# Fp16 spreading of attention weights, and a first expert chunk that is weighted later, in a one-core attention and expert block on Trainium2

## The reference

```python
# neighbourhood attention, 16 heads of 8 channels, 13 neighbours (K)
qkv = (x @ qkv_w.T + qkv_b)...;  q, k, v = qkv[0] * SCALE, qkv[1], qkv[2]
attn = einsum('bhld,bhlkd->bhlk', q, k[:, :, nbr, :]) + rpb[:, bidx][None]
attn = softmax(attn, axis=-1)
out = einsum('bhlk,bhlkd->bhld', attn, v[:, :, nbr, :]) @ proj_w.T + proj_b
# experts: a GRU with 1024 states over the 512 steps gives the routing vectors
routing = l2norm(hs.reshape(B, S, E, D));  expr = (x @ expr_w.T).reshape(B, S, E, D)
gram = einsum('bsed,bsfd->bsef', routing, routing);  diff_n = l2norm(gram - eye(E))
penalty = mean(sum(diff_n ** 2))
cos_dist = 1 - sum(expr * routing) / (|expr| * |routing|)
scores = cos_dist * (1 + penalty)
top_v, top_i = top_k(scores, 2);  mult = softmax(top_v)
moe = sum over e of weight[e] * (silu(x @ gate_w[e].T) * (x @ up_w[e].T)) @ down_w[e].T
out = moe + the same form with the shared weights
```

## Time and profile before

| | us |
|---|---|
| median of 3 runs | 4211.66 |
| lowest, highest | 4198.45, 4226.81 |
| the profiled execution | 4216.87 |
| its span (first to last instruction) | 4215.0 |

### The profile page before, as it was taken

The page is one execution under the profiler, slowest core; times in us unless marked ns, Lnnn a source line. Parts: engine busy times, 40 slices in busy tenths (PEclk is TensorE's granted clock), DMA queues, the critical chain, the costliest instruction groups (busy, mean ns, idle before and its releaser), DMA issues. The chain is left out here.

```text
span 4215.0 us, 179359 instructions
## 1 busy us (share of the span) xinstructions
PE 3881.9 (92%) x76838; PEld 2507.1 (59%) x76838; DVE 3103.6 (74%) x14963; ACT 1509.4 (36%) x5111; POOL 161.7 (4%) x399
## 2 busy tenths in 40 slices
PE   3999589999999999999999999999999999987999
PEld 3777455656665666566665665656666656654665
DVE  2688677777777777777777777777777777776555
ACT  1112333333333444333333333333333334432222
POOL 1221000000000000000000000000000000000000
PEclk9899789999999999999999999999999999988999
DMA  2010400000000000000000000000000000010000
GB/s 67 18 37 35 155 3 3 3 3 3 3 3 3 3 3 3 3 3 3 3 3 3 3 3 3 3 3 3 3 3 3 3 3 3 3 36 8 10 10 12
DMA packets 46472, 51.44 MB, mean 12 GB/s; under 512 B 11668, under 2 KB 39572, under 8 KB 45716
## 3 DMA queue, kind: packets, MB, share of 16 engines
q1 hardware_dynamic: 45716, 40.48, 3.1%
HBM read 36.28 MB, written 4.19 MB: 10 GB/s over the span
## 5 line engine op out<-in xcount | busy, mean ns | idle before, releaser
L886 PE MATMUL psum<-room,h_parts 128*32 128x384 f16 x65536 | 2770.7, 327 | 137.5 <-DVE h_parts L1015 137.5
L886 PEld LDWEIGHTS psum<-room,h_parts 128*32 128x32 f16 x65536 | 1663.9, 97 | 1161.0 <-DVE h_parts L1015 359.9
L971 DVE STREAM_TRANSPOSE turned<-psum 128x128 f32<-128x128 f32 x1024 | 323.6, 316 | 524.2 <-PE psum L886 524.2
L1075 ACT ACTIVATE r_by<-gates 128x32 f32<-128x32 f32 x1024 | 253.2, 247 | 1154.3 <-DVE gates L950 1154.3
L747 DVE CUSTOM_DVE_ANT_0 products<-routes 128x128 f32<-128x128 f32 x1855 | 478.4, 270 | 5.0 <-ACT routes L740 3.0
L998 DVE TENSOR_TENSOR_SCAN state<-w_by,state 128x96 f32<-128x96 f32 x1024 | 366.4, 358 | 129.3 <-ACT state L1081 0.7
L1084 ACT ACTIVATE state<-state 128x32 f32<-128x32 f32 x1024 | 255.3, 249 | 434.7 <-DVE state L998 434.7
L989 DVE TENSOR_TENSOR_SCAN pre_n<-r_by,n_terms 128x96 f32<-128x96 f32 x1024 | 366.5, 358 | 22.9 <-ACT r_by L1075 2.3
L950 DVE TENSOR_TENSOR gates<-turned 128x32 f32<-128x32 f32 x2048 | 375.2, 183 | 0.0
L981 DVE STREAM_TRANSPOSE n_terms<-psum 128x128 f32<-128x128 f32 x1024 | 332.6, 325 | 0.0
L1081 ACT ACTIVATE state<-pre_n 128x32 f32<-128x32 f32 x1024 | 258.7, 253 | 136.6 <-DVE pre_n L989 3.4
(11 more groups left out here) (157 smaller groups left out, 2661.5 us busy)
## 6 DMA issues: line engine op xcount, KB each, us to landing
xs_room<-in_L_ffn_gru_w_hh_dram SPq DMA_DIRECT2D x16, 1536.0 KB, 7.1
room<-in_L_attn_x_dram SPq DMA_DIRECT2D x8, 256.0 KB, 5.4
x_scratch<-room SPq DMA_DIRECT2D x8, 256.0 KB, 2.3
room<-x_scratch SPq DMA_DIRECT2D x32, 64.0 KB, 2.2
out_dram<-room SPq DMA_DIRECT2D x32, 64.0 KB, 2.0
xs_room<-in_L_ffn_gru_w_ih_dram SPq DMA_DIRECT2D x3, 512.0 KB, 5.5
xs_room<-in_L_ffn_gate_w_dram SPq DMA_DIRECT2D x2, 512.0 KB, 6.1
xs_room<-in_L_ffn_up_w_dram SPq DMA_DIRECT2D x2, 512.0 KB, 4.5
```

The lines of the kernel that those rows point to most:

```text
L886: last = nc.tensor.matmul(psum[32 * j:32 * j + 32, bank_of(k, half), 0:3 * P], h_parts[:, q, c, :], w_hh_s[:, s, half, 4 * c + j, :, :].re ...
L971: nc.vector.transpose(turned[:, half, 0, :], gate_bank(k, half, 0)).then_inc(r_turned[half], 1)
```

## The change

*Attention.* `spread` is an fp16 matrix with four groups and the value 1/4096. After the softmax DVE also multiplies the reciprocal sums by 4096; ACT copies the weights to fp16 (the high part), DVE subtracts that copy from them and writes the remainder as fp16 (the low part). 13 neighbours x 2 parts x 16 heads are transposed in four groups of 128 rows (the last has 32) by 16 fp16 transposes, copied out by three copies, and spread by one fp16 matmul per neighbour, which adds both parts. The transposes now stand behind `project(11)` and wait for the low part. `x2` has a place of its own.

*Experts.* The block between is gone. SP loads the weights expert by expert, three DMAs each, two experts during the recurrence, the others at the start of the experts' block. PE, ACT and DVE do the end of the recurrence's tiles, the weights and the first chunk in one list: PE transposes expert `e+2` behind expert `e`'s units. The first chunk uses two unit slots instead of three, and its outputs are copied by ACT to `y_first`. The dot products of the last tile and the scoring, cut into nine pieces, stand between the `hid` multiplies. In the second chunk DVE weights the nine kept outputs in two groups, then takes the statistics. Later chunks are as before.

```diff
-        spread = sb("spread", [P, P // HEADS, P])
+        spread = sb("spread", [P, 4, P], F16)
...
-                nc.gpsimd.affine_select(out=sv, in_=sv, compare_op=ALU.not_equal, fill=1.0, base=0,
-                                        pattern=[[-HEADS, P // HEADS], [-1, HEADS], [0, HD]],
+                nc.gpsimd.affine_select(out=sv, in_=sv, compare_op=ALU.not_equal, fill=1.0 / PSCALE, base=0,
+                                        pattern=[[-2 * HEADS, 4], [-1, HEADS], [0, HD]],
+                                        channel_multiplier=1).then_inc(spread_hi, 1)
+                pool.wait_ge(spread_hi, 1)
+                nc.gpsimd.affine_select(out=sv, in_=sv, compare_op=ALU.not_equal, fill=1.0 / PSCALE, base=-HEADS,
...
-        pT = [carve(L), carve(L)]
+        NGRP = (K + 3) // 4
+        prob_parts = carve(TPS * K * HEADS).bitcast(F16).rearrange("p (t k s h) -> p t k s h", t=TPS, k=K, s=2)
+        pT = carve(NGRP * L // 2).bitcast(F16).rearrange("p (g l) -> p g l", g=NGRP)
         att = carve(TPS, C)
-        x2 = carve(TPS, C)
+        x2 = sb("x2", [P, TPS, C])[:, :, :]
...
+                        nc.vector.tensor_scalar(total[:, :, :], total[:, :, :], PSCALE, None, ALU.mult)
+                        dve.drain()
                         nc.vector.tensor_tensor(probs, probs, total[:, :, :].unsqueeze(2).to_broadcast([P, TPS, K, HEADS]),
                                                 ALU.mult).then_inc(probs_done, 1)
                     value_product(11)
+                    if has_s:
+                        dve.wait_ge(probs_hi, s + 1)
+                        nc.vector.tensor_tensor(prob_parts[:, :, :, 1, :], probs, prob_parts[:, :, :, 0, :], ALU.subtract).then_inc(probs_lo, 1)
...
+                        act.wait_ge(probs_done, s + 1)
+                        nc.scalar.copy(prob_parts[:, :, :, 0, :], probs).then_inc(probs_hi, 1)
...
-                        nc.scalar.copy(pT[0], psum[:, PT_BANK, :])
-                        nc.scalar.copy(pT[1][0:WIN - P, :], psum[0:WIN - P, T_BANK, :]).then_inc(pT_done, 1)
+                        nc.scalar.copy(pT[:, 0:2, :], pT_bank[0])
+                        nc.scalar.copy(pT[:, 2, :], pT_bank[1][:, 0, :])
+                        nc.scalar.copy(pT[0:2 * HEADS, 3, :], pT_bank[1][0:2 * HEADS, 1, :]).then_inc(pT_done, 1)
                         projected(2, vT)
...
-                            half, rows = (0, P) if j < P // HEADS else (1, WIN - P)
-                            nc.tensor.matmul(psum[:, j % 3, :], spread[0:rows, j % (P // HEADS), :], pT[half][0:rows, :],
+                            rows = 2 * HEADS * min(4, K - j // 4 * 4)
+                            nc.tensor.matmul(psum[:, j % 3, :], spread[0:rows, j % 4, :], pT[0:rows, j // 4, :],
                                              start=True, stop=True).then_inc(spread_ps, 1)
...
                     project(10)
+                    project(11)
                     if has_s:
-                        pe.wait_ge(probs_done, s + 1)
+                        pe.wait_ge(probs_lo, s + 1)
                         if present(c):
                             pe.wait_ge(xn2T_done, c + 1)
                         else:
                             pe.wait_ge(qkv_done, 3 * s + 2)
                         for t in range(TPS):
-                            row = probs[:, t, :, :].rearrange("p k h -> p (k h)")
-                            nc.tensor.transpose(psum[:, PT_BANK, t * P:(t + 1) * P], row[:, 0:P], ident[:, :])
-                            last = nc.tensor.transpose(psum[0:WIN - P, T_BANK, t * P:(t + 1) * P], row[:, P:WIN], ident[:, :])
+                            row = prob_parts[:, t, :, :, :].rearrange("p k s h -> p (k s h)")
+                            for g in range(NGRP):
+                                at, end = g * P, min((g + 1) * P, 2 * WIN)
+                                last = nc.tensor.transpose(pT_bank[g // 2][0:end - at, g % 2, t * P:(t + 1) * P], row[:, at:end], ident_16[:, :])
                         last.then_inc(pT_ps, 1)
-                    project(11)
                     project(12)
...
+        EARLY_W = 2
+        ew_in = [sem(f"ew_in{e}") for e in range(NE)]
+        x_words = (L + 2) * B
+        raw_room = [xs_room[:, x_words + e * 6 * P:x_words + (e + 1) * 6 * P] for e in range(EARLY_W)]
+        raw_room += [xs_room[:, e * 6 * P:(e + 1) * 6 * P] for e in range(NE - EARLY_W - 2)]
+        def load_expert(sp, e):
+            g, u, d = (gate_w[e], up_w[e], down_w[e]) if e < NEXP else (sgate_w, sup_w, sdown_w)
+            w = raw_room[e].rearrange("p (m k) -> p m k", k=P)
+            sp.dma_start(w[:, 0:FC, :], g.rearrange("(f p) k -> p f k", p=P)).then_inc(ew_in[e], 16)
+            sp.dma_start(w[:, FC:2 * FC, :], u.rearrange("(f p) k -> p f k", p=P)).then_inc(ew_in[e], 16)
+            sp.dma_start(raw_room[e][:, 2 * FC * P:], d).then_inc(ew_in[e], 16)
...
+                for e in range(EARLY_W):
+                    load_expert(sp, e)
...
+        y_first = carve(NE, BANK)
+        y_kept = sem("y_kept")
+        def over_chunks(eng, first, second, body):
+            first()
+            second()
+            with eng.Fori(0, NT // QT - 2) as i:
+                body(i + 2)
+        def unit_bank(u, first):
+            return 2 * (u % (2 if first else RING))
+        def turned_bank(e):
+            return 2 if e == 0 else 4
...
+                def turn_weights(e):
+                    pe.wait_ge(ew_in[e], 48)
+                    if e >= 2:
+                        pe.wait_ge(ew_out, e)
+                    for m in range(6):
+                        last = nc.tensor.transpose(psum[:, turned_bank(e) + m // 3, (m % 3) * P:(m % 3 + 1) * P],
+                                                   raw_room[e][:, m * P:(m + 1) * P], ident[:, :])
+                    last.then_inc(ew_tr, 1)
+                def unit(toks, u, first):
+                    e, f = u // FC, u % FC
+                    for k in range(2):
+                        last = nc.tensor.matmul(psum[:, unit_bank(u, first) + k, :], expT[:, e, FC * k + f, :], toks,
+                                                start=True, stop=True)
+                    last.then_inc(gate_ps, 1)
+                def down(i, e):
+                    pe.wait_ge(hid_done, UNITS * i + FC * (e + 1) + RING)
+                    pe.wait_ge(down_read, NE * i + e + (2 if e == 0 else 1))
+                    for t in range(QT):
+                        for f in range(FC):
+                            last = nc.tensor.matmul(psum[:, 6 + e % 2, t * P:(t + 1) * P],
+                                                    hid[(FC * e + f) % (2 * FC)][:, t * P:(t + 1) * P],
+                                                    expT[:, e, 4 + f, :], start=(f == 0), stop=(f == FC - 1))
+                    last.then_inc(down_ps, 1)
+                def first_chunk():
+                    state_products(pe).then_inc(last_ps, 1)
+                    expr_products(NEXP - 2)
+                    expr_products(NEXP - 1).then_inc(expr_ps, 1)
+                    turn_weights(0)
+                    pe.wait_ge(last_read, 1)
+                    turn_weights(1)
+                    for e in range(NE):
+                        pe.wait_ge(ew_out, e + 1)
+                        for f in range(FC):
+                            pe.wait_ge(hid_done, FC * e + f + 2)
+                            unit(xn2T[:, 0:BANK], FC * e + f, True)
+                        if e + 2 < NE:
+                            turn_weights(e + 2)
+                        if e >= 1:
+                            down(0, e - 1)
+                    down(0, NE - 1)
...
+                def keep_weights(e):
+                    act.wait_ge(ew_tr, e + 1)
+                    for h in range(2):
+                        last = nc.scalar.copy(expT[:, e, 3 * h:3 * h + 3, :].rearrange("p m k -> p (m k)"),
+                                              psum[:, turned_bank(e) + h, 0:3 * P])
+                    last.then_inc(ew_out, 1)
+                def keep_output(e):
+                    act.wait_ge(down_ps, e + 1)
+                    nc.scalar.copy(y_first[:, e, :], psum[:, 6 + e % 2, :]).then_inc(down_read, 1)
+                def first_chunk():
+                    act.wait_ge(last_ps, 1)
+                    act.wait_ge(last_dots, 1)
+                    state_copy(0, 4)
+                    state_copy(4, 5)
+                    state_copy(NEXP, 4)
+                    act.wait_ge(expr_ps, NT + 1)
+                    expr_copies().then_inc(last_read, 1)
+                    keep_weights(0)
+                    keep_weights(1)
+                    for e in range(NE):
+                        silu(0, FC * e, True)
+                        if e == 4:
+                            length_roots(act)
+                        if e == 6:
+                            row_roots(act)
+                        if e == 8:
+                            gap_exps(act)
```

(91 more changed lines are left out.)

290 lines of the change are left out of this document (116 added, 174 removed).

## The result

The changed kernel takes 4271.57 us (median of 4 runs, 4246.86 to 4281.88), the kernel before 4212.27 beside it: ratio 1.0117, 95% interval 1.0072 to 1.0162. It is slower, by a little over 1%. The forecast was 4259.

The account below looks back on a forecast made before the run. PE was taken to bound the kernel, busy 92% of the span, mostly in the unedited recurrence. 4216.87 + 70.6 (attention) - 23 (expert end) = 4264.5 us, 4259 at the median's level; range 4165 to 4290.

Parts of the forecast that it names:

- low rounds: Attention's scoring rounds (projection, spread, two keys' scores) at the 1.2 GHz level: 5.59 us each, against 2.91 at full clock.
- the burst: 24 score records on PE ahead of attention's scoring rounds, 2.75 us, forecast to make the clock fall.
- Falls with the burst in each interval: Attention: clock low until scoring ends, 56 us per interval instead of 43.6, +74.4 over six; this case's chance 0.45.
- The full-clock interval: Attention, one score addition to the next with the clock full throughout: 42.0 us.
- T: End of the softmax's normalizing multiply in attention; from scores to the next T forecast at 10.4 us.
- T to the burst: Attention's weight parts, transposes, copies and projections after T: keys start at T+12.0, the burst 2.3 later at full clock.
- the full-clock rival: Attention: rounds keep PE busy, the clock stays full, intervals of 42.0 us; total 4163 us; chance 0.22.
- The first interval and the last sequence: Attention's two ends: first interval, already low, -2.3 us; last sequence, without scores and bound by DVE, -1.5 us.
- The parts of the weights: Splitting attention's weights: high copy on ACT 0.90 us; on DVE low subtraction 1.03, small multiply 0.15 with its drain.
- The expert end: After the recurrence: experts start earlier, first-chunk scoring ends about 31 us earlier, second chunk loses 8.5; -23 us.
- Mixed: Rival in attention: the burst fells the clock in three of six intervals, +28.6 us; total 4217 us; chance 0.22.
- The clock stays full: The full-clock rival: the burst does not fell attention's clock; attention -25.6 us; chance 0.22.

Follow-up runs that it names:

- attention alone: The kernel before with only the attention's part of the change, its experts' part left as it was: 4290.01 us, ratio 1.0157.
- experts alone: The kernel before with only the experts' part of the change, its attention left as it was: 4188.88 us, ratio 0.9956.
- The chain alone: The kernel before plus small multiply, high copy, low subtraction and PE's wait, project(11) moved ahead, parts written but unread: 4234.11 us, ratio 1.0048.

## Why the prediction was right

**Direction and mechanism held.** The forecast named the clock as the largest term, with low rounds from the burst until scoring was over. The rounds measured 5.55 us at the low level (230.51 to 236.06) against 5.59 forecast and 2.90 at full clock (406.77 to 409.67) against 2.91.

**How often.** "Falls with the burst in each interval" was too strong for the profiled execution: four of six, at 57.9 us on average (56 forecast), two at 44.5. The six intervals cost +59.05 instead of +74.4. It was right for attention alone (six of six), and the changed kernel's other runs, longer by 22 to 35 us, point the same way. The price of a low interval was 2 to 3 us too small (57.9 here and 58.8 with attention alone, for 56). That the median came within 12.6 us is in part luck: the profiled execution is 17.6 below its forecast of 4264.5, because two intervals escaped, and the median is above 4259, where the price counts more.

**The full-clock interval** was put at 42.0 and is 44.5. The burst to the end of scoring is right (17.36 against 2.75 + 14.5 + 0.1), and so is the time to T: the normalizing multiply ends at 386.15, 10.4 after 375.75. The term that was too small is T to the burst, 14.3 forecast (12.0 + 2.3), 16.7 measured (386.15 to 402.88):

```profile
386.88 2.08 PE L546 MATMUL psum<-wqp,room 128*128 128x128 f32 x8 [2.99 <-DVE room L348]
388.75 2.71 PE L598 MATMUL psum<-ident,room 128*128 128x128 f16 x16
```

PE had stood still for 2.99 us, and its clock was low (0.50) for the moved project(11) and into the transposes. These, forecast at 0.9 from a rate, take 1.79 even at full clock (212.98 to 214.77); for each of them fp16 wins nothing, since experts alone starts its fp32 ones 0.11 us apart (226.16, 226.27), and there are twice as many now. With 42.0 too low by 2.5 in each of six intervals, the full-clock rival's 4163 was out of reach; the changed kernel with its scores two by two took 4175 to 4194, median 4189.9.

**The first interval and the last sequence:** -1.7 against -2.3; from the last score addition to L749 -2.9 against -1.5, but this stretch is 4.9 us shorter with experts alone, which has the old attention, so nothing follows from it.

**The parts of the weights.** Hi copy 0.89, lo subtraction 1.03, small multiply 0.20 (0.90, 1.03 and 0.15 forecast). The chain alone cost 20 us between medians, where 2 us in each of seven intervals are 14; two of its profiled intervals were low, but the count above gives no ground to lay them on the chain (3 falls at 7 bursts with it, 12 at 21 without).

**The expert end:** 24.5 won, 23 forecast. First chunk 78.5 us (3820.49 to 3898.99) against 79.2, second 54.6 against 55.5, and PE waits for the hidden multiplies there, as forecast (6.01 us ahead of 3895.46).

**The rivals.** "Mixed" (three of six) was closer to the profiled execution's count, four, than the forecast's six, and its reason, something that the program doesn't set, stands in part: the bursts at 226.19 and 402.88 come from the same code behind the same wait, and only the first felled the clock. What the program does set is whether it can happen: with the scores grouped two by two it did not in any profile. "The clock stays full" failed at the burst, which felled the clock with PE busy.

## What to carry to other kernels

Before making PE's work lighter, look at the granted clock beside every window where PE is bound: if small matmuls there stand beside a few large ones, the large ones may be what brings the clock back, and making them lighter can cost more than they took. When such a stage is slow, first break up runs of small matmuls (one line here, 2% in the fp16 kernel), and price a lightened stage at both levels. And when work is deferred, deal it out one piece per free slot: the same nine pieces cost 7.6 us in two lumps and nothing one by one.

## What the runs showed of the hardware that was not expected

- The stream of the light rounds holds either clock level for as long as it lasts: 27.28 us at 0.51 and 17.36 us at 1.00, PE busy in all of both. The fp32 rounds did too: 30.55 us at 0.50.
- Matmuls that only repeat others made the kernel faster: 8 x 13 x 3 more spreads, 4219 us; 8 x 13 x 1, 4202; 8 x 7, all in one round of a sequence, 4206; none, 4272.
- Most of the kernel before's own scatter (4191 to 4251 us in 29 runs) hangs on the burst: without it 12 runs lie between 4204.2 and 4211.7, none of them as short as the lowest with it.
- What in a burst drops the clock at one place and not at another (402.88 did not, 226.19 did) was not tried apart, and stays open. So does why a spread issued four times keeps it up when the fp32 one of the same 0.86 us does not.
